# Placing the norms, projections and sums of a two-layer convolution and attention block anew along its scan rows

## The reference

```python
xn = rmsnorm(x)                                    # over channels
def mamba(x):                                      # x: L=1024 x C=384
    u, z = split(x @ in_proj.T)
    u = silu(causal_conv4(u) + b)
    dt, Bm, Cm = split(u @ x_proj.T)
    delta = softplus(dt @ dt_proj.T + dt_b)
    h[t] = exp(delta * A) * h[t-1] + delta * u * Bm     # 16 states a channel
    y = (h * Cm).sum(states) + u * D
    return (y * silu(z)) @ out_proj.T
g = (mamba(xn) + flip(mamba(flip(xn)))) * scale_mod
x = x + res_scale * (g + sigmoid(depthwise3x3(xn) + b) * xn)
x = x + Wo(attention(layernorm(x)))
x = x + proj(gelu(fc(layernorm(x))))
```

## Time and profile before

| | us |
|---|---|
| median of 3 runs | 4692.39 |
| lowest and highest | 4690.68 and 4701.69 |
| the profiled execution | 4673.44 |
| its span, first to last instruction | 4671.6 |
| busy in it: VectorE, TensorE, POOL, ScalarE | 3704.0, 3489.4, 2900.8, 2534.4 |

### The profile page before, as it was taken

One profiled execution on the slowest core, in us unless ns is written; L12 is line 12 of the kernel. 1 busy time (PEld: TensorE's weight loads), 2 busy tenths in 40 slices (PEclk: granted clock), 3 DMA queues, 4 the chain that ended last, 5 costly groups with the idle time before them and its releaser, 6 DMA issues.

```text
span 4671.6 us, 40161 instructions
## 1 busy us (share of the span) xinstructions
PE 3489.4 (75%) x11626; PEld 1767.2 (38%) x11626; DVE 3704.0 (79%) x2673; ACT 2534.4 (54%) x3563; POOL 2900.8 (62%) x1740
## 2 busy tenths in 40 slices
PE   6300887779777887778877697777877788777797
PEld 2100335523353234533355233542345333452372
DVE  4899679878899878988799787888789988998121
ACT  4433456565565665655565655646556555665262
POOL 3798567656676657665677566666576756776000
PEclk9655888879898888879888798888888888888898
DMA  3999488885788578884888857787687857887100
GB/s 89 207 248 247 104 188 198 199 199 123 183 193 207 139 172 195 184 206 120 187 197 204 194 133 179 180 192 175 148 194 183 211 137 163 206 195 177 45 6 14
DMA packets 224024, 785.11 MB, mean 168 GB/s; under 512 B 25292, under 2 KB 40958, under 8 KB 223518
## 3 DMA queue, kind: packets, MB, share of 16 engines
q0 software_dynamic: 117504, 427.87, 47.2%
q1 hardware_dynamic: 106270, 354.32, 23.9%
HBM read 339.60 MB, written 39.85 MB: 81 GB/s over the span
## 4 chain that ended last, share of the span: by engine, by line
PE 33%; DVE 26%; issue 17%; ACT 10%; POOL 7%; DMA 5%; DVEq 0%; SPq 0%; ACTq 0%; POOLq 0%
DVE pBC L1119 15%; PE pW L549 7%; DMA y<-hb 5%; POOL hb L1297 5%; PE pW L444 5%; PE pW L513 3%; PE pW L481 3%; DVE stat L1158 3%; PE pW L463 3%; PE pW L628 3%; PE pW L493 2%; DVE xres L1079 2%; ACT prob L948 2%; ACT pBC L771 2%; DVE hb L1128 1%
## 5 line engine op out<-in xcount | busy, mean ns | idle before, releaser
L1119 DVE TENSOR_TENSOR_SCAN pBC<-pBC,hb 128x1024 f32<-128x1024 f32 x768 | 1756.7, 2287 | 165.9 <-ACT pBC L771 123.9
L1311 POOL DMA_DIRECT2D y<-hb x792 | 780.9, 989 | 1058.3 <-DVE hb L1128 1013.3
L1297 POOL TENSOR_TENSOR hb<-du_f,b_row 128x1024 f32<-128x1024 f32 x384 | 1042.6, 2737 | 169.2 <-DVE du_f L1086 130.5
L1297 POOL TENSOR_TENSOR hb<-uc_b,b_row 128x1024 f32<-128x1024 f32 x384 | 1018.8, 2654 | 19.1 <-DMA y<-hb 18.9
L1128 DVE TENSOR_TENSOR hb<-pBC,c_row 128x1024 f32<-128x1024 f32 x768 | 940.1, 1224 | 46.5 <-DVE pBC L1119 2.7
L771 ACT ACTIVATE pBC<-delta,vec 128x1024 f32<-128x1024 f32 x384 | 428.4, 1117 | 347.2 <-DVE hb L1128 347.1
L771 ACT ACTIVATE pBC<-xres,vec 128x1024 f32<-128x1024 f32 x384 | 426.5, 1117 | 251.7 <-DVE hb L1128 250.7
L628 PE MATMUL pW<-area,pt 128*128 128x64 f32 x3456 | 441.8, 282 | 156.4 <-ACT pt L938 156.4
L628 PEld LDWEIGHTS pW<-area,pt 128*128 128x128 f32 x3456 | 413.0, 196 | 215.0 <-ACT pt L938 206.7
L1158 DVE TENSOR_REDUCE stat<-pW 128x1 f32<-128x640 f32 (+7 forms) x361 | 257.7, 750 | 215.5 <-PE pW L552 214.0
L513 PE MATMUL pW<-area,consts 128*128 128x512 f32 x288 | 147.7, 664 | 362.6 <-ACT area L983 325.2
(11 more groups left out here) (162 smaller groups left out, 5083.6 us busy)
## 6 DMA issues: line engine op xcount, KB each, us to landing
y<-hb POOLq DMA_DIRECT2D x792, 512.0 KB, 6.6
b_row<-bc_rows SPq DMA_DIRECT2D x256, 512.0 KB, 5.4
c_row<-bc_rows SPq DMA_DIRECT2D x256, 512.0 KB, 4.7
area<-in_x SPq DMA_DIRECT2D x8, 1536.0 KB, 12.9
kept_residual<-in_x SPq DMA_DIRECT2D x8, 1536.0 KB, 17.4
kept_residual<-du_f POOLq DMA_DIRECT2D x24, 512.0 KB, 11.5
xres<-kept_residual SPq DMA_DIRECT2D x8, 1536.0 KB, 14.9
out_x<-xa SPq DMA_DIRECT2D x8, 1536.0 KB, 8.1
```

The costliest lines, as they stand in the source:

```text
L1119: dve.tensor_tensor_scan(flow(d, buf), flow(d, buf), flow(d, hb[slot(r)][:, :]), 0.0, ALU.mult, ALU.add).then_inc(scan_done, 1)
L1297: pool.tensor_tensor(hb[q % NHB][:, :], du[d][:, k, :], b_row[g % 2][:, :], ALU.mult)\
L1311: pool.dma_start(y[:, k, :], hb[q % NHB][:, :], accum_op=ALU.add).then_inc(y_in[k], 16)
```

## The change

- **Depthwise convolution.** VectorE does all three channel tiles: 18 steps for tiles 0 and 1 in turn, then nine for tile 2. `tap` and POOL's additions are gone. The sigmoids of tiles 0 and 1 come before the narrow copies, that of tile 2 behind the first direction's logarithms, with a table load ahead and one behind. `local` (the multiply by the normed input) goes tile by tile, and so do `soft_sum` and `times_u`. `finish` of output tiles 2 to 5 stands behind the last `times_u`.
- **Second softplus in PSUM.** Each channel tile of the second direction uses the banks of pT in turn: absolute value, exp and log at rows 15, 17 and 19, sum and product with u on VectorE at 16, 18 and 20 (the product replaces POOL's multiply), the copy of delta to xres at 17, 19 and 21. The skips move to rows 9 to 11. The projections therefore use two banks of pW beside the rows.
- **The plan.** Each norm is five items in rows of their own. Projections stand at rows 15 to 21, scores and values at 22 to 61, Wo at 63 to 66, the second norm at 67 to 71, the MLP at 72 to 93 with gelu one row behind its product. The next input is loaded at row 62 (behind the values), squared at 63 into du_f, averaged at 66 and normed at 70.
- **Input projection.** It no longer waits for row 95's norm but for the second MLP sum (row 93); ScalarE's copies of u come before the silu of z.

```diff
-VK = KT - 1
...
+FRONT = ([("proj", t, 2.0 if t < 12 else 1.6) for t in range(NPJ)]
+         + [x for p in range(NG + 1) for x in (("scores", p, 3.7), ("values", p, 3.7))]
+         + [("ctx_t", g, 0.8) for g in range(6)] + [("next_square", 0, 0.0)] + [("wo", t, 2.0) for t in range(6)])
+R0, R1 = 15, 66
+RS = 12
...
-        dt_bank = [pBC[0], pBC[1], pS, pT, pS, pT]
+        dt_bank = [pBC[0], pBC[1], pS, pT, pT, pT]
...
-                elif (kind, n) == ("ln_var", 1) and more:
-
-                    sp.wait_ge(ln_var, at(4, a, 4))
+                elif (kind, n) == ("ctx_t", 0) and more:
+
+                    sp.wait_ge(pv_done, at(NG, a, NG))
                     load_next(b + 1)
...
+                        pe.wait_ge(x2_ready, at(2, b - 1, 0))
...
+            def gates(b, lo, hi):
+
+                for k in range(lo, hi):
+                    act.wait_ge(dw_step, at(9 * KT, b, 17 + k if k < 2 else 27))
+                    act.activation(gate[:, k, :], gate[:, k, :], ACT.Sigmoid).then_inc(sig_ready, 1)
...
                     soft_exp(b, 1, n)
-
+                    soft_log(b, 1, n)
+                elif kind == "step_copy" and early:
+
+                    act.wait_ge(du_ready, at(6, b, 4 + n))
                     act.wait_ge(xa_ready, at(6, b, 0))
-                    act.activation(delta[1][:, n, :], dt_bank[KT + n][:, :], ACT.Relu).then_inc(relu_done, 1)
-                elif kind == "step_log" and not early:
-                    for k in range(KT):
-                        soft_log(b, 1, k)
+                    act.copy(delta[1][:, n, :], dt_bank[KT + n][:, :]).then_inc(delta_ready, 1)
...
+                    gates(b, 2, 3)
+                    act.preload_act_table_set(LOG_EXP)
...
+            def times_u1(b, k):
+
+                dve.wait_ge(sum_ready, at(3, b, k + 1))
+                dve.wait_ge(yd_ready, at(6, b, 6))
+                dve.tensor_tensor(du[1][:, k, :], dt_bank[KT + k][:, :], uc[1][:, k, :], ALU.mult).then_inc(du_ready, 1)
...
+            def local(b, k):
+
+                dve.wait_ge(sig_ready, at(3, b, k + 1))
+                acc = gate[:, k, :].rearrange("p (h w) -> p h w", w=WW)
+                dve.scalar_tensor_tensor(out=acc, in0=acc, scalar=rs_col, in1=xnp[:, k, 1:1 + HH, 1:1 + WW],
+                                         op0=ALU.mult, op1=ALU.mult).then_inc(loc_ready, 1)
...
-                    depthwise(b, 0, 18)
+                    depthwise(b, 0, 22)
+                    local(b, 0)
+                    depthwise(b, 22, 24)
+                    local(b, 1)
+                    depthwise(b, 24, 27)
                     for k in range(KT):
...
+                        if k == 2:
+                            local(b, 2)
+                        elif layer1:
+                            finish(b - 1, k)
+                        soft_sum(b, 0, k)
+                        times_u(b, k)
                     if layer1:
-                        for t in range(3):
+                        for t in range(2, 6):
                             finish(b - 1, t)
...
-                    for j in range(1, 9):
-                        pool.wait_ge(dwt_ready, at(9, b, j + 1))
-                        pool.wait_ge(dwp_step, at(8, b, j - 1))
-                        pool.tensor_tensor(gate[:, VK, :], gate[:, VK, :], hb[3 + j % 2][:, :], ALU.add)\
-                            .then_inc(dwp_step, 1)
```

More of the change, by code:

```diff
@@ new lines, in mlp, with spread @@
+def mlp(c, r):
+    return [x for q in range(NFG) for x in (("mlp", c * (NFG + 1) + q, r + 2 * q), ("gelu", c * (NFG + 1) + q, r + 2 * q + 1))] + [
+        ("mlp", c * (NFG + 1) + NFG, r + 2 * NFG), ("mlp_out", c, r + 2 * NFG), ("mlp_add", c, r + 2 * NFG + 1)]
+def spread():
+    left, at, out = sum(w for _, _, w in FRONT), float(R0), []
+    for kind, n, w in FRONT:
+        if (kind, n) == ("scores", 0):
+            at = max(at, out[-1][2] + 1)
+        out.append((kind, n, int(at)))
+        at += w * (R1 - at) / max(left, 1e-9)
+        left -= w
+    return out
@@ L1025, in iteration @@
                             item(kind, i, b, False)
[L1026 to L1028 removed]
+                    if more:
+                        if not layer1:
+                            item("next_square", 0, b, True)
+                            item("next_mean", 0, b, False)
+                        for t in range(6):
+                            copy_u(b + 1, t)
                     silu_z(b)
[L1030 to L1031 removed]
                 else:
```

231 lines of the change are left out of this document (91 added, 140 removed).

## The result

| | before | after |
|---|---|---|
| median, us | 4696.84 | 4882.71 |
| lowest and highest of 4 runs each | 4690.68 and 4701.69 | 4870.07 and 4884.64 |
| span of the profiled execution | 4671.6 | 4882.2 |
| ratio, 95% interval | | 1.0391 [1.0367, 1.0414] |

What follows compares the result with a forecast made beforehand. VectorE was busiest (79%), but limits differed by stretch: VectorE in attention, TensorE before the first row. Six samples +198, step 0 to 1 +14.3 and the ends gave +210.3, span 4881.9; plus 20.8, 4903 us (4790 to 5020).

Steps and rivals of the forecast that it cites:

- Context and Wo: Rows 62 to 66: 44 us (37 to 50), +14.1, with a 14.0 us stall at row 64 for the load.
- Between samples: From the end of row 95 to the next sample's first scan: 85.5 us, +14.3 (bounds +9 to +17).
- the landing: Tile 2's accumulating DMA to kept_residual, between samples: taken at 10.3 us, with `times_u` of tile 2 waiting for it.
- T: Time mark in the prediction: the end of row 95, 2689.1 us in sample 4 before the change.
- Rival 1: Between samples: the kept_residual transfer lands as fast as the page says, 3.2 us; whole 4853 us, chance 0.07.
- Rows to the first scores: Rows 0 to 21: 132 us (124 to 142), -4.8, with TensorE's projections in rows 15 to 21 holding VectorE.
- R: Time mark in the prediction: the first scan of a sample.
- The rows that the prediction named as a sign: Projection rows, 15 to 21: 7 to 9 us each, with VectorE waiting for decays.
- Attention: 27 groups in 40 rows instead of 42: VectorE work 170.5 plus waits 18.5, 189 us (184 to 198), -4.4.
- Second norm: Second norm, MLP input and split, rows 67 to 73, with the next norm: 45 us (41 to 52), +12.9.
- MLP and end: Rows 74 to 95: work 79.7 plus waits 4.3 at the two sums, 84 us (81 to 90), +0.9.
- Rival 3: Faster: projections fit beside their rows, row 22 at 99.4 us after the first scan, row 63 hides the load; 4623 us, 0.11.

Runs made afterwards that it cites:

- The first experiment: Changed kernel with the three squares of the next sample, and ScalarE's wait for its load, moved from row 63 to row 66; 4787.68 us, ratio 1.0212.

## Why the prediction was right, and where it was so by luck

The forecast span missed the measured one by 0.3 us, and that is luck. The span of the kernel before lay 20.8 us below its median, and the forecast carried these 20.8 us over to 4903; the span after, 4882.2 us, lies only 0.5 us below the median. So the change costs 210.6 us by the spans, where the forecast had 210.3, but 185.9 us by the medians above, and 200 to 204 us against the later medians of the kernel before. By parts of the program (the first scans of samples 0, 1 and 7 come at 120.0, 578.7 and 4061.2 us, before at 114.6, 571.4 and 3862.4):

| part | forecast | measured |
|---|---|---|
| lead of sample 0 | +4 | +5.4 |
| sample 0, with the step to sample 1 | +4.3 | +1.9 |
| samples 1 to 6 | +198 | +191.5 |
| sample 7 and tail | +4 | +11.8 |
| sum | +210.3 | +210.6 |

- **Context and Wo (44, measured 43.4).** Right in mechanism and size: the decay of row 64 was 13.6 us late (forecast 14.0), the load landed in 12.7 us (12.9), and Wo came behind it. The first experiment undid it.
- **Between samples (85.5, measured 79.9).** Right up to the landing: the logarithms ended at T + 55.1 (forecast 54.9), `local` at T + 60.2 (59.8), with the depthwise steps in cover, as the run with one tap showed. The mis-sized term is the landing, taken at 10.3 us and measured at 5.4 here, 5.2 and 5.3 at the other seven. The 24 landings of the earlier trace rows were those of transfers with two neighbours and with loads under way beside them; the run with three in a row took the loads away and left the neighbours. I had read the shortest of the 24 as that of a lone one. The Trainium skill ("DMA: Bandwidth & Descriptors", Anatomy of one DMA) gives, by 2.0 us plus bytes over 436 GB/s, an estimate of 3.2 us; the trace stands between, nearer to it than to my value. Rival 1 priced a landing of 3.2 us at 50 us of the whole; the landing as measured was worth 4.9 x 7 = 34 us. The output tiles behind the product took 9.1 us (forecast 9.0), and from the last of them to the first scan it was 3.6 us instead of 5.1. So `times_u` waited 4.65 us, where the prediction had named some 9 as a sign, and the first scan came 80 us after T instead of 85.
- **Rows to the first scores (132, measured 139.6).** The mechanism is right: TensorE holds the stretch, and the pad's wait, which the prediction didn't see, only replaces part of it. Two terms were too small. The projections began at R + 69.1 instead of 66.6. They took 65.6 us with the step sizes instead of 58.9. The step sizes took 8.65 us instead of 5.2: 3.75 for the first, behind 9.35 us of idling, then 1.98 and 2.92. TensorE stops 1.68 us twice for ScalarE's copy of delta, and the projections themselves, which in the earlier trace rows had 53.7 us with short stops at a granted clock of 0.95, were busy for 54.0 us at 0.85. The rest was 1.6 shorter. The rows that the prediction named as a sign, of 7 to 9 us each, came as 3.5 to 19.2 us.
- **Attention (189, measured 190.4).** Work of 170.9 us (forecast 170.5) and waits of 19.5 (18.5).
- **Second norm (45, measured 46.7).** Work with the next norm in it was 40.4 us (42.2), the waits 6.3 (2.8). Of the norm's three products one took 3.08 us, beside GpSimd's multiply, and the other two 2.47 together.
- **MLP and end (84, measured 80.4).** Only 1.5 us of waits remained where I had kept 4.3, and the work was 0.8 less. That gelu in rows of its own ended the other waits is argued; no run moved it alone.
- **The sum.** Minus 5.6, minus 3.6 and minus 0.6 against plus 7.6, plus 1.4 and plus 1.7: single terms were off by up to 8 us a sample, and they cancelled, as the parts did (sample 7 was 8 us short, six samples 6.5 over). So the 15 us a sample that the range allowed was nearer to what the working could tell than the 0.3 us. Rival 3, the faster one, decided at whether the projections fit beside their rows; they took 65.6 us where it had 32. A time like its 4623 us came only once the plan gave them 14 rows, the load its time and the output tiles another place: 4563 us.

## What to carry to other kernels

When work of one engine is laid beside rows of another, count both sides of every stretch: a stretch whose rows are shorter than the work beside them wastes the rows' engine, and each row moved there is free until the two sides are equal (here from 7 to 14 rows, 24 us a sample in the two stretches; from 14 to 17 rows nothing). Put the consumer of a load as many rows behind its issue as the load takes, or the wait stands in the queue in front of things that are due. The longest wait in a trace may be worth nothing: ask what is late next before it is removed. A DMA's time from a trace holds for the traffic that it ran beside: look at its neighbours and at the other queue before it is used as that of a lone one.
